# Attention projections as three fp16 products of high and low halves, with the second group's query masks on POOL

## What is computed

```
x = x + 0.5 * ffn(layernorm(x))     # 12 experts, the best 3 of each row, 256 -> 640 -> 256
x = x + attn(layernorm(x))          # 16 heads of 16 columns, chunks of 128 rows
x = x + 0.5 * ffn(layernorm(x))     # the same weights again

# attn:
qkv = x @ w_qkv.T + b_qkv           # q, k, v, each 256 wide
# for each sequence, chunk by chunk, with a state S (16 x 16) per head:
inter  = (q * decay_q) @ S
scores = (q @ k.T) * dmask          # causal decay in the chunk
out    = inter + scores @ v
S      = lam_c * S + (k * decay_k).T @ v
# result: out @ w_out.T + b_out
```

## Time and profile before

| | |
|---|---|
| median of 3 runs | 795.31 us (795.23 to 799.47) |
| the profiled execution | 794.92 us, of which its span is 793.1 us |
| mean granted clock of TensorE in the span | 0.898 |
| busy: PE, PEld, DVE, ACT, POOL | 628.5, 549.7, 493.3, 330.9, 370.9 us |
| attention stage | from about 352 to 484 us of the span |

### The profile page before, as it was taken

How to read it: one execution, slowest core, us unless ns; L and a number is a source line. 1 busy time by engine, 2 the same in 40 slices (tenths; PEclk the granted TensorE clock), 3 DMA queues, 4 the chain that set the end, 5 groups by cost and what they waited for, 6 DMA issues and landing times.

```text
span 793.1 us, 21180 instructions
## 1 busy us (share of the span) xinstructions
PE 628.5 (79%) x7596; PEld 549.7 (69%) x7597; DVE 493.3 (62%) x1033; ACT 330.9 (42%) x934; POOL 370.9 (47%) x258
## 2 busy tenths in 40 slices
PE   1414677999999997559999997129999999999853
PEld 1313666998999997137888885028999999999711
DVE  6897896554454454068898988973544555455405
ACT  2977986444434443013232323026444444444300
POOL 0004166888888885101101000023888888888510
PEclk9756899999999999669999997558999999999967
DMA  9995723465665443810000003003444444444383
GB/s 300 374 371 173 219 43 52 95 126 112 132 125 114 92 74 41 232 53 2 2 0 0 0 2 107 1 27 121 67 75 73 77 70 71 74 71 72 48 231 106
DMA packets 72583, 79.79 MB, mean 101 GB/s; under 512 B 6304, under 2 KB 64928, under 8 KB 72160
## 3 DMA queue, kind: packets, MB, share of 16 engines
q0 software_dynamic: 22656, 30.95, 23.8%
q1 hardware_dynamic: 49888, 48.35, 18.7%
HBM read 48.08 MB, written 31.20 MB: 100 GB/s over the span
## 4 chain that ended last, share of the span: by engine, by line
PE 62%; DVE 16%; issue 7%; ACT 5%; DMA 5%; SPq 3%; ACTq 1%; DVEq 1%; POOL 0%; POOLq 0%
PE PS L810 59%; PE PS L867 3%; ACT A L715 2%; DMA expert_sums<-A,place 2%; DVE W L1222 2%; DVE A L1374 2%; DMA W<-w 1%; SPq L450 1%; DMA A<-expert_sums 1%; ACT A L597 1%; DVE A L1371 1%; DVE A L1575 1%; ACT W L605 1%; ACT A L641 1%; SPq L452 1%
## 5 line engine op out<-in xcount | busy, mean ns | idle before, releaser
L810 PE MATMUL PS<-A,W 128*128 128x128 f16 (+1 forms) x3796 | 247.6, 227 | 16.3 <-DVE W L1222 12.0
L810 PEld LDWEIGHTS PS<-A,W 128*128 (+1 forms) x3796 | 238.9, 107 | 22.7 <-DVE W L1222 12.9
L527 POOL DMA_INDIRECT A<-xn_rows,token x118 | 162.7, 1379 | 184.1 <-DVE token L1397 124.1
L810 PE MATMUL PS<-W,A 128*128 (+1 forms) x1898 | 236.9, 280 | 6.9 <-DVE A L1443 3.5
L545 POOL DMA_INDIRECT expert_sums<-A,place x118 | 194.9, 1652 | 73.8 <-issue 40.3
L715 ACT ACTIVATE A<-PS,b1s 128x128 f32<-128x128 f32 x590 | 159.2, 391 | 157.7 <-PE PS L810 157.7
L810 PEld LDWEIGHTS PS<-W,A 128*128 128x128 f16 (+1 forms) x1898 | 191.3, 104 | 33.9 <-issue 5.4
L1433 DVE CAST A<-A 128x1280 f16<-128x1280 f32 x58 | 50.0, 861 | 191.8 <-ACT A L715 191.8
L810 PE MATMUL PS<-A 32*128 32x128 f32 (+3 forms) x1248 | 65.9, 282 | 32.1 <-DVE A L1374 24.9
L1435 DVE TENSOR_TENSOR A<-A 128x1280 f16<-128x1280 f32 x58 | 86.6, 1493 | 2.0
L810 PEld LDWEIGHTS PS<-A 32*128 32x128 f32 (+3 forms) x1248 | 52.0, 150 | 43.8 <-DVE A L1374 29.8
(11 more groups left out here) (161 smaller groups left out, 423.9 us busy)
## 6 DMA issues: line engine op xcount, KB each, us to landing
W<-w SPq DMA_DIRECT2D x24, 640.0 KB, 11.1
A<-expert_sums SPq DMA_DIRECT2D x16, 512.0 KB, 7.3
expert_sums<-zeros SPq DMA_DIRECT2D x2, 2304.0 KB, 18.6
expert_sums<-zeros SPq DMA_DIRECT2D x12, 384.0 KB
xn_rows<-A SPq DMA_DIRECT2D x8, 512.0 KB, 6.9
A<-b SPq DMA_DIRECT2D x2, 1536.0 KB, 7.7
X<-x SPq DMA_DIRECT2D x4, 512.0 KB, 6.0
out<-X SPq DMA_DIRECT2D x8, 256.0 KB, 2.6
```

Source lines behind the costliest of these rows:

```text
L527: nc.gpsimd.indirect_dma_start(XG[q][:, u * D:(u + 1) * D], None, xn_dram[:, :], bass.IndirectOffsetOnAxis(ap=token[:, at:at + 1], axis=0) ...
L810: return nc.tensor.matmul(out_, l, r, start=start, stop=stop_, skip_group_check=True)
```

## The change

Four things are done:

- The weights of the queries, keys and values are scaled by one power of two and cut into fp16 halves, once, in a new step `attention_weights` between `blocks` and `combine` of the first stage. ScalarE takes the squares and cuts the high parts, TensorE sums over the partitions, VectorE finds the factor and cuts the low parts.
- The transposed rows are cut too: ScalarE's copy becomes the high part XTh, and a new VectorE step `low_columns`, at the head of each tile's work, makes the low part XTl. TensorE's projections wait for it. Each projection is three fp16 products in place of one fp32 product.
- The factor is undone where the projections leave PSUM: as a scale of ScalarE's evictions, and in the values' addition on VectorE, which becomes two instructions of 128 columns.
- QE and QO of the second group and QD go from VectorE to POOL, behind its addition of the output bias, with a semaphore `a_q1` of their own. ScalarE's eviction waits in addition for `a_q`.

```diff
@@ POOL, in the loop over t, behind the addition of bo_s
+                        pool.wait_ge(a_qk, t * 4 + 4)
+                        pool.sem_inc(pool_held, 1)
+                        nc.gpsimd.tensor_scalar(QE[:, 1], QR[:, 1], const("even"), None, ALU.mult)
+                        nc.gpsimd.tensor_scalar(QO[:, 1], QR[:, 1], const("odd"), None, ALU.mult).then_inc(a_q1, 1)
+                        nc.gpsimd.tensor_tensor(QD, QR, const("decay_q").rearrange("p (g c) -> p g c", g=G),
+                                                ALU.mult).then_inc(a_qd, 1)
@@ ScalarE
+            def attention_weights():
+                act.wait_ge(attn_w_in, 16 * 9)
+                flat = "p k n -> p (k n)"
+                nc.scalar.activation(junk[:, 0:KC * 2 * D], wqk_s.rearrange(flat), ACT.Square,
+                                     accum_out=attn_ss[:, 0:1]).then_inc(a_w_squares, 1)
+                act.wait_ge(a_w_squares, 1)
+                nc.scalar.activation(junk[:, 0:KC * D], wv_s.rearrange(flat), ACT.Square,
+                                     accum_out=attn_ss[:, 1:2]).then_inc(a_w_squares, 1)
+                act.wait_ge(a_w_scaled, 1)
+                nc.scalar.mul(wqk_h[:, :, 0, :], wqk_s, attn_scale[:, 0:1]).then_inc(a_w_hi, 1)
+                act.wait_ge(a_w_lo, 1)
+                nc.scalar.mul(wv_h[:, :, 0, :], wv_s, attn_scale[:, 0:1]).then_inc(a_w_hi, 1)
...
-                    nc.scalar.copy(XTa[b % 2], bank[4][:, 0:D].rearrange("p (k c) -> p k c", k=KC)).then_inc(a_xt, 1)
+                    nc.scalar.mul(XTh[b % 2], bank[4][:, 0:D].rearrange("p (k c) -> p k c", k=KC),
+                                  X_SCALE).then_inc(a_xh, 1)
...
+                    act.wait_ge(a_q, t + 1)
                     act.wait_ge(a_qd, t + 1)
                     for n, dst in ((0, QR[:, 0]), (2, KT[:, 0]), (1, QR[:, 1]), (3, KT[:, 1])):
                         nc.scalar.activation(dst, bank[4][:, n * P:(n + 1) * P], ACT.Identity,
-                                             bias=bqk_s[:, n:n + 1]).then_inc(a_qk, 1)
+                                             bias=bqk_s[:, n:n + 1], scale=attn_back[:, :]).then_inc(a_qk, 1)
@@ TensorE
+            def attention_weights():
+                pe.wait_ge(a_w_squares, 2)
+                matmul(bank[5][:, 0:2], ones[:, :], attn_ss[:, :], True, True).then_inc(a_w_normed, 1)
...
                     pe.wait_ge(a_xt, t + 1)
                     for n in range(4):
+                        i = 0
                         for k in range(KC):
-                            ins = matmul(bank[4][:, n * P:(n + 1) * P], wqk_s[:, k, n * P:(n + 1) * P],
-                                         XTa[b % 2][:, k, :], k == 0, k == KC - 1)
+                            for part, columns_ in ((0, XTh), (0, XTl), (1, XTh)):
+                                ins = matmul(bank[4][:, n * P:(n + 1) * P], wqk_h[:, k, part, n * P:(n + 1) * P],
+                                             columns_[b % 2][:, k, :], i == 0, i == 5)
+                                i += 1
...
                     for k in range(KC):
-                        matmul(bank[5][:, 0:D], XTa[b % 2][:, k, :], wv_s[:, k, :], k == 0, k == KC - 1)
+                        for part, columns_ in ((0, XTh), (1, XTh), (0, XTl)):
+                            matmul(bank[5][:, 0:D], columns_[b % 2][:, k, :], wv_h[:, k, part, :], i == 0, i == 5)
+                            i += 1
...
-                    pe.wait_ge(a_q, t * 2 + (g + 1))
+                    if g == 0:
+                        pe.wait_ge(a_q, t + 2)
+                    else:
+                        pe.wait_ge(a_q1, t + 1)
@@ VectorE
+            def attention_weights():
+                v = nc.vector
+                dve.wait_ge(a_w_normed, 1)
+                step(v.tensor_reduce(attn_back[:, :], bank[5][:, 0:2], AX.X, ALU.add))
+                step.settle()
+                bits = iscl[:, 0, :]
+                power_of_two(attn_back[:, :], slice(0, 1), bits[:, 0:1], bits[:, 1:2])
+                step(v.tensor_scalar(attn_scale[:, :].bitcast(I32), bits[:, 0:2], 23, None, ALU.logical_shift_left))
+                step.settle()
+                step(v.tensor_scalar(attn_back[:, :], attn_scale[:, 1:2], 1.0 / X_SCALE, None, ALU.mult))
+                step.settle()
+                dve.sem_inc(a_w_scaled, 1)
+                for n, (raw, cut) in enumerate(((wqk_s, wqk_h), (wv_s, wv_h))):
+                    dve.wait_ge(a_w_hi, n + 1)
+                    v.scalar_tensor_tensor(cut[:, :, 1, :], raw, attn_scale[:, 0:1], cut[:, :, 0, :], ALU.mult,
+                                           ALU.subtract).then_inc(a_w_lo, 1)
...
-                    for g in range(G):
-                        dve.wait_ge(a_qk, t * 4 + (2 * g + 2))
-                        v.tensor_scalar(QE[:, g], QR[:, g], const("even"), None, ALU.mult)
-                        v.tensor_scalar(QO[:, g], QR[:, g], const("odd"), None, ALU.mult).then_inc(a_q, 1)
-                    v.tensor_tensor(QD, QR, const("decay_q").rearrange("p (g c) -> p g c", g=G),
-                                    ALU.mult).then_inc(a_qd, 1)
+                    dve.wait_ge(a_qk, t * 4 + 2)
+                    v.tensor_scalar(QE[:, 0], QR[:, 0], const("even"), None, ALU.mult)
+                    v.tensor_scalar(QO[:, 0], QR[:, 0], const("odd"), None, ALU.mult).then_inc(a_q, 1)
+
+                def low_columns(t, b):
+                    dve.wait_ge(a_xh, t + 1)
+                    v.scalar_tensor_tensor(XTl[b % 2], bank[4][:, 0:D].rearrange("p (k c) -> p k c", k=KC), X_SCALE,
+                                           XTh[b % 2], ALU.mult, ALU.subtract).then_inc(a_xt, 1)
...
-                    v.tensor_tensor(V2m[:, :, 0:4:3, :], bank[5][:, 0:D].rearrange("p (q s d) -> p q s d", s=2, d=HD),
-                                    bv_s.rearrange("p (q s d) -> p q s d", s=2, d=HD), ALU.add).then_inc(a_ve, 1)
+                    for s in range(2):
+                        ins = v.scalar_tensor_tensor(V2m[:, :, 3 * s, :],
+                                                     bank[5][:, 0:D].rearrange("p (q s d) -> p q s d", s=2, d=HD)[:, :, s, :],
+                                                     attn_back[:, :],
+                                                     bv_s.rearrange("p (q s d) -> p q s d", s=2, d=HD)[:, :, s, :],
+                                                     ALU.mult, ALU.add)
+                    ins.then_inc(a_ve, 1)
...
                 def tile(t, b, last=False):
+                    if not (last and b == B - 1):
+                        low_columns(t + 1, b + 1)
                     values_keys(t)
...
+                low_columns(0, 0)
                 queries(0)
                 masked(0, 0)
```

More of the change, by code:

```diff
@@ L269, in build @@
         XNa = [carve(D) for _ in range(2)]
-        XTa = [carve(D).rearrange("p (k c) -> p k c", k=KC) for _ in range(2)]
+        XTh = [carve(D, F16).rearrange("p (k c) -> p k c", k=KC) for _ in range(2)]
+        XTl = [carve(D, F16).rearrange("p (k c) -> p k c", k=KC) for _ in range(2)]
         QR = carve(D).rearrange("p (g c) -> p g c", g=G)
@@ L293, in build @@
         bqk_s = sb("bqk_s", [P, 2 * G])
+        assert xn_at + T * D + KC * 2 * D <= AR
+        wqk_h = A[:, xn_at + T * D:xn_at + T * D + KC * 2 * D].bitcast(F16).rearrange(
+            "p (k s n) -> p k s n", k=KC, s=2)
+        wv_h = extra1[:, 0:KC * D].bitcast(F16).rearrange("p (k s n) -> p k s n", k=KC, s=2)
+        attn_ss = sb("attn_ss", [P, 2])
+        attn_scale = sb("attn_scale", [P, 2])
+        attn_back = sb("attn_back", [P, 1])
         PS = ctx.enter_context(nc.psum_tensor("PS", [P, 8, 512], F32))
@@ L369, in build @@
         dmask_in = sem("dmask_in")
+        a_w_squares = sem("a_w_squares")
+        a_w_normed = sem("a_w_normed")
+        a_w_scaled = sem("a_w_scaled")
+        a_w_hi = sem("a_w_hi")
+        a_w_lo = sem("a_w_lo")
+        a_xh = sem("a_xh")
+        a_q1 = sem("a_q1")
         a_xn = sem("a_xn")
@@ L802, in _ @@
                 blocks(f)
+                if f == 0:
+                    attention_weights()
                 combine(f)
```

7 lines of the change are left out of this document (added).

## The result

The changed kernel takes 800.81 us (median of 7 runs, 800.40 to 803.25) against 796.09 (7 runs, 792.98 to 799.47): 1.0062 times the time before, with a 95% interval of 1.0041 to 1.0083. The profiled execution took 801.95 us, its span 800.1. The forecast was 800.5.

The account below looks back on a forecast made before the run. TensorE's and VectorE's loops were both taken as bounds, closing within 0.05 us. Start 1.5, first tile 0.2, loop 5.4 and end -1.8 sum to +5.3 us, so 800.5 us was forecast, range 796 to 806.5.

Parts of the forecast that it names:

- What bounds: Attention stage loop: TensorE's and VectorE's loops close within 0.05 us, so an edit gains only if it shortens both.
- The removal is worth nothing: Taking QE 1, QO 1 and QD off VectorE, which waits for the scores anyhow: 0, at most 0.17 us per tile.
- The rival that counted the removal in full: Masked product waits for QD, not the scores: -0.40 us per tile, 790.5 to 791 us; chance 0.11.
- The additions to the loop: VectorE's low columns +0.34 and split values' addition +0.20, less 0.05 slack: +0.49 us per tile, +5.4 over eleven tiles.
- POOL's work: QE 1, QO 1 and QD on POOL take 1.4 to 2.2 us, covered before their readers: cost 0.
- POOL holds VectorE up: Rival: VectorE's scale step waits for POOL, say 0.3 us in eleven tiles, +3.3, so 803.9 us; chance 0.18.
- The start: First projection waits for low columns behind the update of X, then runs at half clock: +1.5 us, up to +2.0.
- The first tile: Tile before the eleven loop tiles: only the split of the values' addition counts, +0.2 us, to 0.4.
- The end of the stage: Last tiles, where TensorE sets the time: -0.2 for the first, -0.7 for each of two, -0.2 for the last; -1.8 us.
- The weights: Scaling and splitting the weights before `combine`, in idle time of VectorE and ScalarE: cost 0, without that cover 8 us.
- the clock: Rival: TensorE's stalls of over 1 us per tile lower its clock, some 5 us a tile, 60 in all; chance 0.04.
- the gaps: Rival: new instructions vanish in VectorE's idle gaps, 0.9 us per tile, so 795 us, no change; chance 0.17.

Follow-up runs that it names:

- halves alone: Changed kernel with all masks and QD back on VectorE; 802.72 us, 1.0091 times the kernel before.
- POOL's masks alone: Kernel before with only the second group's masks and QD moved to POOL, projections still fp32; 1.0035 times the kernel before.
- one count: POOL's masks alone, with both groups' masks counted on `a_q` again, so POOL also waits for VectorE's masks; steady tile 8.12 us, stage 140.87 us.
- early low columns: Changed kernel with the first tile's low columns made between the second and third piece of the update of X; 1.0077 times the kernel before.
- factor as a number: Changed kernel with ScalarE's evictions of queries and keys taking the factor as a program number, not an SBUF column; stage 139.55 us.
- POOL's low columns: Halves alone, with the low columns made by subtraction on POOL from a scaled fp32 copy that ScalarE adds; 1.0014 times the kernel before.

## Why the prediction was right, and where it was not

**What bounds.** That two loops close within 0.05 us of each other held where it was tried: 0.52 us more on VectorE made the tile 0.45 longer (halves alone). With VectorE relieved, TensorE's loop showed as the bound, but in a kernel where it had been made longer, so the slack on that side was not measured by itself.

**The removal is worth nothing.** Right, and shown by halves alone: 0.94 us from QO to the masked product with the three instructions, 1.01 without them in the changed kernel. The rival that counted the removal in full fell with it.

**The additions to the loop.** Low columns 0.34 forecast, 0.32 to 0.33 measured; the split 0.20 forecast, 0.18 to 0.19 measured. The loop's mean rose by 0.529 for 0.49 forecast: +5.8 us for +5.4. That this fits so well owes something to chance: halves alone raise the mean by 0.37, and the other 0.16 is the move to POOL, which the sum put at nothing.

**POOL's work.** Here the step failed that looked only at who reads POOL's masks. Those readers did have their cover. What it cost stood elsewhere: the bias sum, pushed behind the masks, holds VectorE's scale step, and the scores start later. The first is the rival "POOL holds VectorE up". Its mechanism is shown: in the changed kernel the step ends at 413.58 and the sum at 413.55, with POOL's masks alone at 408.32 and 408.30, with one count at 411.84 and 411.83. The Trainium skill, "SBUF — State Buffer", section "SBUF: two separate sides", has the port pair that VectorE and GpSimd share as an exclusive lock. These ends agree with it. The price of the hold was 0.13 in the kernel with POOL's masks alone, 0.3 as forecast or more only with one count, and in the tile shown of the changed kernel 0.03 (residual 0.23 behind the step's start for 0.20), since the late VectorE meets only the sum's end. In the loop's other tiles it was 0.04 at most, but for the first of them (0.33); the mean is 0.05. The larger part is the scores: they start 0.13 or 0.24 us behind QO's end, by turns of two tiles, and the masked product 1.01 or 1.12 behind it for 0.94 in halves alone, a mean of 0.12 more. Together that is about the 0.16. The later scores are shown to hang on the count (0.05 with one count); in the three last tiles, which are written out, they start 0.10 behind QO's end before the change and after it. The step of TensorE's sequencer that takes the time was not isolated.

**The start.** +1.5 forecast, +1.46 measured, and the early low columns show the cause.

**The first tile.** +0.2 forecast, +1.55 and +1.26 measured in the two profiles. The step took VectorE for its bound, but TensorE ran at half clock through 6.1 of the tile's 8.72 us, and 5.4 of 8.43. At full clock, with the factor as a number, the tile was 0.53 shorter than before (the number itself may have a part in that, as it has 0.16 in the last tiles). The prediction let the late rise touch the first scores only; it can cover most of a tile. Since the rise also came late without the halves (one count), it was not shown that the change causes it.

**The end of the stage.** -1.8 forecast, -0.2 measured: the step that failed most in this kernel. Three things were left out. The first of the last tiles, which still has residual and scales of the loop ahead of it, stayed with VectorE: +0.60 where -0.2 stood. The next two gained 0.39 each and not 0.7: TensorE's products are shorter by 0.75 (0.55 in the projections as forecast, and 0.86 to 0.66 from the values' first product to the transposes), but the evictions and the copy behind them delay the output projection by 0.18, and the state product waits 0.21 for the keys. The rows of one such tile of the changed kernel:

```profile
475.41 1.50 ACT L677 ACTIVATE A<-PS,bqk_s,attn_back 128x128 f32<-128x128 f32 x4 [3.19 <-PE PS L848]
...
477.23 1.13 PE L848 MATMUL PS<-W,A 128*128 128x256 f32 x4
...
480.58 2.79 PEld L848 LDWEIGHTS PS<-A 128*128 128x128 f32 x60 [0.21 <-DVE A L1661]
```

The rows of such a tile before:

```profile
466.95 1.14 ACT L641 ACTIVATE A<-PS,bqk_s 128x128 f32<-128x128 f32 x4 [3.75 <-PE PS L810]
...
468.59 1.13 PE L810 MATMUL PS<-W,A 128*128 128x256 f32 x4
```

The output projection starts 1.82 us behind the eviction; before, 1.64. The factor as a number gave back 0.16 of it. The cost per eviction was never worked out: the prediction spoke of the factor on VectorE and not of the one on ScalarE. The Trainium skill, "ScalarE: Activation LUTs", section "What ACT_TABLE_LOAD costs", adds about 93 ns to such an instruction for each operand that is a column. The 88 measured here agree with it. Of the last tile's -0.2, 0.03 was seen.

**The weights, the clock, the gaps.** The weights were hidden. The clock did not fall in the loop. VectorE's idle time behind its own statistics was no room for new work: the low columns cost their whole pitch.

**The sum.** By the terms the stage should have grown by 5.3 us and grew by 8.6, nearly all of the difference in the first tile and the last ones; the medians differ by 4.7, the profiled executions by 7.0. The steps between these are on record: outside the stage the profile after is 1.55 us shorter than the one before, which makes 7.1 of the 8.6; and the profiled execution before was 1.17 us under its median, the one after 1.14 above, which makes 4.7 of the 7.0. So the forecast time is nearer than its working, and that it came so near is luck: its terms missed the stage by 3.3 us. What makes the executions differ is not shown. The clock may have a part: an execution whose first tile takes 6.64 and not 8.72 is 2.1 us shorter. But the program outside the stage also varies (span less stage is 657.8 to 661.8 us over the eleven profiles of kernels that leave nothing out), and which executions of the changed kernel had an early rise was not seen. That part stays open.

## What to carry to other kernels

Where two engines' loops close within a few hundredths of a microsecond, work taken off one is worth nothing by itself, and work added to the later one counts nearly in full; find in one tile which wait ends last, and price every instruction that comes in there. An operation moved to a free engine has a third cost beside its length and its readers: what stood behind it in that engine's queue now runs later and can meet another engine's work. A reader that must wait on a count of its own can start later too: in the changed kernel that was the larger cost. A factor that becomes an operand need not be free: look for the instructions that it lengthens.

## What was not expected of the hardware

- The clock's rise at the start of the stage: three profiles with the same first projection had it directly behind that, 7.0 us behind the update's start, or only 12.5 and 13.2 us behind it in spite of more work in between. Their first tiles took 6.64, 8.43 and 8.72 us, of which the factor as a number may explain some 0.16. Two others with one and the same first projection had it at 6.0 and 13.3.
- ScalarE's eviction of 128 columns takes 456 ns with a bias and a factor as columns, 368 with the factor as a number.
- POOL's multiplication of 128 columns by a factor per partition takes 0.60 us, nearly as long as its product over 256 (0.64) and its sum (0.72).
- POOL's low columns and VectorE's update were both longer where they overlapped, 0.92 us for 0.67 later on and 4.22 for the 3.81 of the changed kernel:

```profile
353.14 4.22 DVE L1591 SCALAR_TENSOR_TENSOR X<-A,gate,X 128x768 f32<-128x768 f32 x4
...
355.62 0.92 POOL L589 TENSOR_TENSOR A<-A 128x256 f16<-128x256 f32 x1 [3.75 <-ACT A L669]
...
363.53 0.67 POOL L589 TENSOR_TENSOR A<-A 128x256 f16<-128x256 f32 x1 [5.15 <-ACT A L669]
```
